# Last cross-attention of a two-layer decoder: the order of weightings and maxima within a slot on TensorE and VectorE

## The reference

```python
q = lat @ Wq + bq
kv = concatenate([x, lat], axis=1) @ Wkv + bkv        # x: the 77 media rows
k, v = split(kv, 2)
sim = einsum('bhid,bhjd->bhij', q * scale, k)
sim = sim - max(sim, axis=-1)
attn = softmax(sim, axis=-1)
out = einsum('bhij,bhjd->bhid', attn, v)
return out @ Wout + bout
```

## Time and profile before

| | us |
|---|---|
| median of 3 runs | 1122.23 (1119.28 to 1124.82) |
| the profiled execution | 1122.65 |
| its span, first to last instruction | 1120.9 |
| PE busy, whole span | 1043.4 (93%) |
| DVE busy | 738.5 (66%) |
| ACT busy | 503.5 (45%) |
| POOL busy | 248.6 (22%) |

### The profile page before, as it was taken

The page is one execution under the profiler, slowest core; times in us unless marked ns, Lnnn a source line. Parts: engine busy times, 40 slices in busy tenths (PEclk is TensorE's granted clock), DMA queues, the critical chain, the costliest instruction groups (busy, mean ns, idle before and its releaser), DMA issues.

```text
span 1120.9 us, 18232 instructions
## 1 busy us (share of the span) xinstructions
PE 1043.4 (93%) x6794; PEld 888.2 (79%) x6794; DVE 738.5 (66%) x1736; ACT 503.5 (45%) x933; POOL 248.6 (22%) x308
## 2 busy tenths in 40 slices
PE   6859889999997599999999999999999999999896
PEld 3647678888886478998999999899999899999432
DVE  5867867556566668777767667657676756762257
ACT  4336554333235554544434444435444435443453
POOL 7111400053735222212121111112111111110001
PEclk9969999999999689999999999999999999999998
DMA  7100000000001000000000000000000000000001
GB/s 234 7 1 1 1 1 1 1 1 1 1 1 38 1 1 2 1 2 1 1 2 1 1 1 2 1 2 2 1 2 1 2 1 1 2 1 1 1 1 38
DMA packets 15682, 10.13 MB, mean 9 GB/s; under 512 B 8759, under 2 KB 14827, under 8 KB 15083
## 3 DMA queue, kind: packets, MB, share of 16 engines
q1 hardware_dynamic: 15595, 8.96, 2.8%
HBM read 7.60 MB, written 1.05 MB: 8 GB/s over the span
## 4 chain that ended last, share of the span: by engine, by line
PE 81%; DVE 9%; ACT 4%; POOL 3%; issue 2%; DMA 1%; POOLq 0%; DVEq 0%; ACTq 0%; SPq 0%
PE PS L1458 77%; PE PS L1470 2%; POOL VXA L639 2%; PE PS L1829 1%; DVE BIG L1077 1%; DVE mx L1074 1%; DVE st L983 1%; DVE KB L1287 1%; DVE X_ODD L994 1%; ACT BIG L727 1%; DVE X_EVEN L994 1%; POOL rs L570 0%; ACT XT L727 0%; ACT BIG L757 0%; DMA QB<-crow 0%
## 5 line engine op out<-in xcount | busy, mean ns | idle before, releaser
L1458 PEld LDWEIGHTS PS<-VXA,BIG 128*128 128x128 f32 (+1 forms) x3136 | 400.7, 192 | 26.7
L1458 PE MATMUL PS<-VXA,BIG 128*128 128x65 f32 (+2 forms) x3136 | 395.8, 271 | 0.0
L941 ACT ACTIVATE BIG<-PS 128x512 f32<-128x512 f32 (+1 forms) x320 | 189.8, 593 | 228.9 <-PE PS L1458 228.2
L1343 DVE TENSOR_REDUCE mxm<-PS 128x1 f32<-128x512 f32 x256 | 170.7, 688 | 83.6 <-PE PS L1458 78.7
L1458 PE MATMUL PS<-QA,KA 128*128 128x512 f32 (+1 forms) x320 | 145.4, 454 | 0.3
L1458 PE MATMUL PS<-QB,KB 128*128 128x512 f32 (+1 forms) x320 | 126.1, 394 | 0.0
L1458 PE MATMUL PS<-KA,QA 128*128 128x512 f32 (+1 forms) x512 | 116.2, 330 | 0.7 <-DVE mxm L1343 0.5
L1458 PEld LDWEIGHTS PS<-KA,QA 128*128 128x128 f32 x512 | 87.0, 190 | 21.4 <-DVE mxm L1343 2.3
L673 POOL CAST KA<-KA 64x78 fp32r<-64x78 f32 (+1 forms) x128 | 54.9, 429 | 221.5 <-ACT KA L914 218.0
L914 ACT ACTIVATE KA<-PS,b1s 64x78 fp32r<-64x78 f32 (+1 forms) x128 | 64.3, 502 | 84.5 <-PE PS L1458 82.9
L673 POOL CAST QB<-QA 64x512 fp32r<-64x512 f32 x64 | 39.0, 609 | 257.2 <-ACT QA L914 257.0
(11 more groups left out here) (255 smaller groups left out, 1536.3 us busy)
## 6 DMA issues: line engine op xcount, KB each, us to landing
X_EVEN<-in_x SPq DMA_DIRECT2D x4, 256.0 KB, 3.8
VXA<-in_L_ffn_Wg SPq DMA_DIRECT2D x1, 1024.0 KB, 5.8
VXA<-in_L_ffn_Wu SPq DMA_DIRECT2D x1, 1024.0 KB, 7.7
VXA<-in_L_ffn_Wd SPq DMA_DIRECT2D x1, 1024.0 KB, 9.4
REG<-in_L_xattn_Wkv SPq DMA_DIRECT2D x1, 1024.0 KB, 4.8
QB<-crow SPq DMA_DIRECT2D x64, 2.0 KB
out<-X_EVEN SPq DMA_DIRECT2D x4, 256.0 KB, 2.3
wq1s<-in_L_xattn_Wq SPq DMA_DIRECT2D x1, 512.0 KB, 8.3
```

What stands on the lines that cost most here:

```text
L941: act.activation(PX[0:rows, g % 4, :], PS[0:rows, g % 2, :], ACT.Exp, scale=SCALE_W).then_inc(pw_ready, 1)
L1343: dve.tensor_reduce(mxm[:, p % 2, h, m:m + 1], PS[:, 2 + g % 2, :], AX.X, ALU.max).then_inc(mu_free, 1)
L1458: return pe.matmul(dst, lhsT, rhs, start=start, stop=stop, **kw)
```

## The change

Two places are exchanged, in two of the three hand-written loops. TensorE issues the weighting of the slot behind directly after the slot's score, and the next pair's units after it. VectorE runs the slot's reductions after `head_out` and `lo`, no longer before them. ScalarE's program is as before, and so are all instructions and waits.

```diff
@@ VectorE's loop
                 for slot in range(SLOTS):
-                    if p + 1 < PAIRS:
-                        for u in MAX_UNITS.get(slot, []):
-                            maxima(p + 1, u)
                     if slot == 0 and p:
                         head_out(2 * p - 1)
                     if slot == KB:
                         head_out(2 * p)
                     for key, h in splits(tasks, slot - 1):
                         lo(key, h)
+                    if p + 1 < PAIRS:
+                        for u in MAX_UNITS.get(slot, []):
+                            maxima(p + 1, u)
                     if (p, slot) in NORM_STEPS:
@@ TensorE's loop
                 for slot in range(SLOTS):
                     s_wide(p, slot)
+                    if SLOTS * p + slot:
+                        pv(SLOTS * p + slot - 1)
                     if p + 1 < PAIRS:
                         for u in MAX_UNITS.get(slot, []):
                             max_unit(p + 1, u)
-                    if SLOTS * p + slot:
-                        pv(SLOTS * p + slot - 1)
                     for key in tasks.get(slot, []):
```

## The result

| | before | after |
|---|---|---|
| median of 4 runs (us) | 1123.42 | 1143.24 |
| lowest to highest | 1119.28 to 1124.82 | 1141.59 to 1146.01 |
| profiled execution | 1122.65 | 1141.59 |
| its span | 1120.9 | 1139.9 |

The account below looks back on a forecast made before the run. The prediction took TensorE's own back-to-back work as the bound. 31 transposition waits of 0.66 us, 20.5 us, on the profiled 1122.65 us made 1143.1, stated as 1143 us, range 1133 to 1151.

Parts of the forecast that it names:

- PE's own work is the bound, so a new wait counts in full: Pipeline: PE waited only 2.4 us in 639 us, so no later idle time can take up a new wait.
- The chain, term by term: Slots 5 and 6: weighting, `head_out`, K's second low half, unit 8's reduction, tail, `cmx`, release; transposition waits 0.66 us.
- Number of waits: Transpositions: `crow` is written 32 times, one in the prologue, so 31 wait.
- What a pair pays: Each pair's transposition: one wait of 0.66 us, bounds 0.48 to 0.85 us.
- The three waits of 0.3 for the transfer of `crow` stay: Next pair's first score: `crow`'s transfer and that score both move 0.6 later, so three 0.3 us waits remain.
- Slack 1.38 us: Transposition in the kernel before: could start at 619.01 after `cmx`, PE came at 620.39, so 1.38 us to spare.
- the prediction's list of what PE waits for: PE's waits in a slot: ScalarE's exponentials, the two unit banks and, in slot 6, `cmx`.
- Weightings earlier, units later in slots 0 to 4: nothing: Slots before 5: weightings 0.2 to 0.6 us sooner after their score, unit banks tight in slots 1 and 2; cost 0.
- Rival B: Slot 2: unit 4 also waits for its bank, 0.1 to 0.3 us a pair; 1146 to 1155 us, chance 0.08.
- Rival D: Whole pipeline: a gap in every pair lowers the granted clock, 24 us once per batch, 1167 us; chance 0.02.

Follow-up runs that it names:

- the run with slot 5 alone: The kernel before with both edits, TensorE's and VectorE's, made in slot 5 only; 1144.43 us, ratio 1.0194.
- the run with the extra reduction in the new order: The changed kernel with one more reduction of unit 8's bank ahead of unit 8's own, once per pair; 1174.13 us, ratio 1.0443.

## Why the prediction was right

- *PE's own work is the bound, so a new wait counts in full*: right. 20.1 us more in the pipeline, 19.9 of waits.
- *The chain, term by term*: weighting to `head_out` 622.65 - 621.61 = 1.04 (1.04 forecast); `head_out` 0.67 (0.67); low half to reduction 624.11 - 623.32 = 0.79 (0.76); reduction to tail 0.61 (0.61); tail to `cmx` 0.50 (0.51); end of `cmx` to load 0.12 (0.12). The wait was 0.67 (0.66). The hold behind a low half, which the rule in the Trainium skill's "VectorE: DVE Perf Modes", section "Two Vector instructions with no wait between them", names, is there again: 0.79 after 0.76, against 0.61 after 0.69.
- *Number of waits*: 30, not 31. In the last pair with units there is no K two pairs on, hence no low half in the chain; its distance grew by 0.18.
- *What a pair pays*: 0.72 against a listed wait of 0.67, so 0.05 more. It goes with the wait and not with TensorE's new order: the other runs show it too (0.22 a pair for a listed 0.17, 1.33 for 1.26), and with the transposition in slot 7, which keeps the new order and has no such wait, a pair is as long as before. Where the 0.05 lies isn't shown. With 30 for 31 the two errors nearly cancel. That 1143 met the median of 1143.24 to 0.3 us is luck beyond this: the executions lie between 1141.59 and 1146.01.
- *"The three waits of 0.3 for the transfer of `crow` stay"*: wrong. They are gone after, and the three pairs with a norm in slot 6 grew only by 0.50, 0.29 and 0.53. The transposition's wait took their place; this gave back about 1 us.
- *Slack 1.38 us*: right for `cmx`, wrong as a statement on the transposition. Its bank, missing from the prediction's list of what PE waits for, was a second condition with no slack. It did not spoil the forecast because the new order on VectorE brings the low half ahead of the reductions, so `cmx` is the later of the two. Had I forecast TensorE's half of the change alone, I would have missed it by 18 us, as its expectation shows (1129 for 1147.49).
- *Weightings earlier, units later in slots 0 to 4: nothing*: right, by the run with slot 5 alone. Rival B's wait at the unit banks came only without TensorE's part.
- *Rival D, the clock*: not in the changed kernel (1.00 in both stretches above), but real where the waits are longer.

## What to carry to other kernels

Where the bound engine has no idle time, look for its nearest wait and retell the slots around it in the new order with start-to-start times from the rows; what counts on the other engine is what is left to do after the last event that it depends on, not how much it does. List **every** semaphore that an instruction waits for, its buffer's release among them: a condition met just when it is needed left no wait in this profile, and made the next harmless-looking edit cost 15 us. And a piece that needs nothing from the late event belongs ahead of it: one exchange of two calls gave back all but 0.3 of the pipeline's 20.1 us.

## What was unexpected of the hardware

The price of a wait on TensorE is not constant. In the changed kernel and in those with waits of up to 0.8 us a pair, a pair costs the same extra time all along (but for the three with a norm in slot 6), and the granted clock is 1.00 in the pipeline's stretches from 415 us on. With waits of 1.3 us a pair the clock fell now and then to the lower of its two levels. Two stretches of the run with the extra reduction in the new order:

```profile
650.00:700.00 50.00, 47.69 (x322) 42.86 (x321) 34.26 (x66) 21.75 (x38) 7.15 (x15) 1.00 0.01 1
700.00:750.00 50.00, 46.56 (x301) 41.96 (x300) 31.72 (x64) 20.07 (x36) 7.00 (x15) 0.93 0.00 1
```

The work is the same pattern of pairs in both; the second has the lower clock (0.93 as a mean) and a PE that is no busier for it. In it the clock is at the lower level for some 7 us, from the wait at a transposition on (the matmul of 725.54, 1.15 us idle before it), and a weighting takes 1.80 instead of 1.00:

```profile
728.00:732.00 4.00, 4.00 (x15) 3.52 (x15) 0.69 (x1) 0.60 (x1) 0.00 (x0) 0.50 0.00 1
...
730.40 1.80 PE L1461 MATMUL PS<-VXA,BIG 128*128 128x65 f32 x8
...
733.02 1.00 PE L1461 MATMUL PS<-VXA,BIG 128*128 128x65 f32 x8
```

In this execution eight pairs were longer by 2.9 to 4.6 us instead of 1.3, 22 us more in all, and it took 1185.42 us where waits alone give 1162; its other executions took 1169.74 to 1175.22 at mean clocks of 0.972 to 0.966. So a forecast by waits was good to 2 us where it had the right waits and the clock stayed up in the pipeline (1143 for 1143.24, 1143 for 1144.43, 1125 for 1125.86, 1125 for 1123.39), and 12 and 27 us too low where the clock didn't. What decides when it falls wasn't tried: the waits of 1.26 us before 725.54 and at 662.04 are much alike, and it fell at the first and stayed up at the second.
